# Gating of the normalised input moved from VectorE to GpSimd in a one-core attention kernel

## What is computed

```python
xn = jax.nn.silu(group_norm(x, gn_scale, gn_offset))
qkv = jnp.einsum('bxyc,cd->bxyd', xn, w_qkv)
q, k, v = jnp.split(qkv, 3, axis=-1)
...
q = q * HEAD_CH ** (-0.5)
sim = jnp.einsum('bhdi,bhdj->bhij', q, k)
attn = jax.nn.softmax(sim, axis=-1)
out = jnp.einsum('bhij,bhdj->bhid', attn, v)
...
out = jnp.einsum('bxyd,dc->bxyc', out, w_out) + b_out
return out + x
```

## Time and profile before

| | |
|---|---|
| device time, median of 3 runs | 3889.32 us (3886.81 to 3890.93) |
| the profiled execution, its device time | 3886.07 us |
| its span, first to last instruction | 3884.3 us |
| mean granted TensorE clock | 0.99 of full speed |
| busy: PE / PEld | 3643.0 us (94%) / 2099.6 us (54%) |
| busy: DVE | 3349.9 us (86%) |
| busy: ACT | 2811.0 us (72%) |
| busy: POOL | 1766.9 us (45%) |
| DMA, queue of the program's transfers | 21.2% of 16 engines' span |

### The profile page before, as it was taken

How to read it: one execution, slowest core, us unless ns; L and a number is a source line. 1 busy time by engine, 2 the same in 40 slices (tenths; PEclk the granted TensorE clock), 3 DMA queues, 4 the chain that set the end, 5 groups by cost and what they waited for, 6 DMA issues and landing times. The chain is left out here.

```text
span 3884.3 us, 92365 instructions
## 1 busy us (share of the span) xinstructions
PE 3643.0 (94%) x32844; PEld 2099.6 (54%) x32844; DVE 3349.9 (86%) x4378; ACT 2811.0 (72%) x3074; POOL 1766.9 (45%) x1739
## 2 busy tenths in 40 slices
PE   4889999999999999999999999999999999998997
PEld 2555555555555555555555555555555555555553
DVE  6888989889898898888888898888988989888885
ACT  3777777777777777777777777777777777777774
POOL 1353544445444444544535444344444444444444
PEclk7999999999999999999999999999999999999999
DMA  2212212132121222213122121221212222131220
GB/s 89 60 30 80 58 49 70 33 88 56 50 78 39 67 56 69 58 39 86 37 80 59 49 69 38 81 56 50 77 39 67 56 69 58 40 85 37 61 61 33
DMA packets 120769, 228.84 MB, mean 59 GB/s; under 512 B 12672, under 2 KB 29056, under 8 KB 120320
## 3 DMA queue, kind: packets, MB, share of 16 engines
q1 hardware_dynamic: 120320, 222.87, 21.2%
HBM read 71.57 MB, written 33.55 MB: 27 GB/s over the span
## 5 line engine op out<-in xcount | busy, mean ns | idle before, releaser
L509 POOL TENSOR_TENSOR Pl<-P,Ph 128x512 f16<-128x512 f32 x1024 | 1238.3, 1209 | 1703.9 <-ACT Ph L623 1691.0
L620 ACT ACTIVATE P<-ST,cns 128x1024 f32<-128x1024 f32 x1024 | 1141.0, 1114 | 899.3 <-PE ST L1108 883.4
L782 DVE TENSOR_REDUCE mx<-TP 128x1 f32<-128x1024 f32 x1024 | 1246.3, 1217 | 164.5 <-PE TP L1019 156.8
L623 ACT ACTIVATE Ph<-ST,cns 128x1024 f16<-128x1024 f32 x1024 | 1133.8, 1107 | 0.0
L835 DVE TENSOR_TENSOR Pl<-P,Ph 128x512 f16<-128x512 f32 x1024 | 978.8, 956 | 11.5 <-ACT Ph L623 7.3
L1137 PE MATMUL PV<-V,Ph 128*128 128x129 f16 (+2 forms) x10240 | 862.1, 210 | 3.9 <-DVE Pl L835 1.4
L1137 PEld LDWEIGHTS PV<-V,Ph 128*128 128x128 f16 x10240 | 772.0, 97 | 124.9 <-ACT pv_sum L631 8.8
L1137 PE MATMUL PV<-V,Pl 128*128 128x65 f16 x8192 | 834.8, 192 | 0.0
L1137 PEld LDWEIGHTS PV<-V,Pl 128*128 128x128 f16 x8192 | 723.0, 98 | 109.1 <-issue 0.6
L1108 PE MATMUL ST<-QK 128*128 128x512 f16 x2048 | 778.2, 380 | 2.6 <-issue 2.6
L1107 PE MATMUL ST<-QK 128*128 128x512 f16 x2048 | 778.6, 380 | 0.2 <-ACT Ph L623 0.2
(11 more groups left out here) (105 smaller groups left out, 2872.8 us busy)
## 6 DMA issues: line engine op xcount, KB each, us to landing
QK<-QK SPq DMA_DIRECT2D x384, 256.0 KB, 4.8
res<-in_x SPq DMA_DIRECT2D x128, 256.0 KB, 2.8
out<-res SPq DMA_DIRECT2D x128, 256.0 KB, 2.0
x_in<-in_x SPq DMA_DIRECT2D x61, 512.0 KB, 3.8
V<-V SPq DMA_DIRECT2D x16, 1040.0 KB, 6.3
V<-in_L_conv_w_qkv SPq DMA_DIRECT2D x4, 768.0 KB, 10.2
P<-in_L_conv_w_out SPq DMA_DIRECT2D x1, 1024.0 KB, 13.9
z<-in_x SPq DMA_DIRECT2D x1, 512.0 KB, 5.6
```

What stands on the lines that cost most here:

```text
L509: nc.gpsimd.tensor_tensor(Pl[:, v % 4, HALF:], P32[:, v % 2, HALF:], Ph[:, v % 4, HALF:], ALU.subtract).then_inc(lo_pool, 1)
L620: nc.scalar.activation(P32[:, v % 2, :], ST[:, slot, :], ACT.Exp, scale=cns[:, 0:1])
L623: nc.scalar.activation(Ph[:, v % 4, :], ST[:, slot, :], ACT.Exp, scale=cns[:, 0:1]).then_inc(exp_done, 1)
L782: nc.vector.reduce_max(mx[:, hh, qb:qb + 1], TP[:], AX.X).then_inc(top_drained, 1)
```

## The change

VectorE no longer takes part in the gating except in the prologue. GpSimd's new `silu` does four operations for each piece, with a semaphore `silu_step` between dependent ones: th = z th; high part of xn = z + th, written as float16; z = z + th, float32; low part = z - high part (this last is what `low_xn` did). `silu_ops(step, u)` deals them out from unit (1,10) on, alternately two and one in a unit: two in even units, one in odd ones, 32 operations in units (1,10) to (2,14). They stand behind `low_probs` and the division in GpSimd's queue. `Z_AT` and `TANH_AT` move to fit, and `silu_tanh` waits for the low part of the piece two before, because `th` is now read until then.

```diff
-Z_AT = [(1, 8), (1, 11), (1, 13), (2, 1), (2, 4), (2, 7), (2, 11), (2, 13)]
-TANH_AT = [(1, 9), (1, 12), (1, 15), (2, 3), (2, 5), (2, 9), (2, 12), (2, 15)]
-SILU_AT = [(1, 11), (1, 13), (2, 0), (2, 4), (2, 7), (2, 11), (2, 13), (3, 0)]
-LOW_XN_AT = [(1, 12), (1, 14), (2, 1), (2, 5), (2, 8), (2, 12), (2, 14), (3, 1)]
+Z_AT = [(1, 8), (1, 10), (1, 13), (1, 15), (2, 2), (2, 5), (2, 7), (2, 10)]
+TANH_AT = [(1, 9), (1, 11), (1, 14), (2, 0), (2, 3), (2, 6), (2, 8), (2, 11)]
+SILU_FROM = (1, 10)
...
+def silu_ops(step, u):
+
+    n = 16 * step + u - 16 * SILU_FROM[0] - SILU_FROM[1]
+    first = 3 * (n // 2) + 2 * (n % 2)
+    return [divmod(k, 4) for k in range(first, first + 2 - n % 2) if 0 <= k < 4 * PIECES]
...
+            def silu(image, par, i, op):
+
+                c, half = i % CC, i // CC
+                n = 3 * PIECES * (image - 1) + 3 * i
+                if op == 0:
+                    pool.wait_ge(silu_ready, PIECES * image + i + 1)
+                    nc.gpsimd.tensor_tensor(th[:, i % 2], z[:, i % 2], th[:, i % 2], ALU.mult).then_inc(silu_step, 1)
+                if op == 1:
+                    pool.wait_ge(silu_step, n + 1)
+                    nc.gpsimd.tensor_tensor(xn[:, par, c, half, 0], z[:, i % 2], th[:, i % 2], ALU.add
+                                            ).then_inc(silu_step, 1)
+                if op == 2:
+                    pool.wait_ge(silu_step, n + 2)
+                    nc.gpsimd.tensor_tensor(z[:, i % 2], z[:, i % 2], th[:, i % 2], ALU.add).then_inc(silu_step, 1)
+                if op == 3:
+                    pool.wait_ge(silu_step, n + 3)
+                    nc.gpsimd.tensor_tensor(xn[:, par, c, half, 1], z[:, i % 2], xn[:, par, c, half, 0],
+                                            ALU.subtract).then_inc(xn_lo, 1)
...
-                    if (s, u) in LOW_XN_AT and not last:
-                        low_xn(b + 1, 1 - par, LOW_XN_AT.index((s, u)))
+                    for i, op in [] if last else silu_ops(s, u):
+                        silu(b + 1, 1 - par, i, op)
...
-                wait(act, xn_f32, PIECES * image + i - 1)
+                wait(act, xn_lo, PIECES * image + i - 1)
...
-                        if (s, u) in SILU_AT:
-                            silu(b + 1, 1 - par, SILU_AT.index((s, u)))
```

More of the change, by code:

```diff
@@ L322, in conv_attention @@
         xn_f32 = sem("xn_f32")
+        silu_step = sem("silu_step")
         xn_hi = sem("xn_hi")
```

## The result

Before ran at 3888.07 us (median of 4), the changed kernel at 3820.22 us (3818.45 to 3822.49, 4 runs): ratio 0.9826, 95% interval 0.9809 to 0.9843. It is faster by 68 us, 1.7%; the forecast was 3833, 56 us less. The profiled execution took 3821.33 us around a span of 3819.6.

The account below looks back on a forecast made before the run. TensorE's work plus its waits, mainly for `ms` behind the port VectorE and GpSimd share, bounds the kernel. Release 6.3 us an image, less GpSimd's load, nets -3.7, times 15 = -56: 3886 - 56 = 3830, plus 3 gives 3833 us; range 3795 to 3905.

Parts of the forecast that it names:

- the gated stretch: Unit (1,10) to the end of (3,1), where the next image is gated; TensorE busy 84.25 of 91.00 us, losing 6.75.
- The rules of the port: Four rules on how VectorE and GpSimd operations delay each other at their shared port; a hand-over costs GpSimd about 0.38 us.
- the fourth: With both queues full, VectorE and GpSimd alternate at the shared port; shown for one tiny operation only.
- Rival 3: GpSimd keeps the port through back-to-back operations, delaying VectorE in even units: slower by 92 us, 3981; chance 0.15.
- The walk: Following VectorE's and GpSimd's queues through the stretch unit by unit with known durations: net -3.7 us an image.
- The price of the release: Taking the gating operations off VectorE shortens shift units and their neighbours by 6.3 us an image at most.
- rival 1: Port not crowded, VectorE's operations find gaps: the full 6.3 us x 15 = 94 us, 3795; chance 0.12.
- Unit (2,9) stays at 4.7: In (2,9), and (2,1) built like it, the transposed output delays VectorE, not gating, so the release gains nothing there.
- The average wait of `ms`: In shift units GpSimd is never idle, so `ms` waits for an operation's end: on average 0.6 us, at most 1.2.
- Rival 2: GpSimd becomes the bound, every operation colliding at 1.54 us: the stretch stays at 91 us, 3889; chance 0.13.
- GpSimd keeps up: A pair of units asks 7.1 us of GpSimd, which has 6.6 plus stalls; it holds, without much to spare.
- recovers at the long units: GpSimd falls behind by up to half a microsecond a pair and catches up at (2,1), (2,5) and (2,9).

## Why the prediction was right

*Where the time was lost, and by what.* Right: the gated stretch, and in it `ms` in the shift units. TensorE's wait for `ms` fell from 98.0 to 75.1 us over the whole run; the changed kernel's row:

```profile
PE TP L1050 <- DVE ms L778: 75.1, 98, 3.0
```

*The rules of the port.* Right, all four; the fourth rested on one four-element operation and now stands on full-size ones. VectorE's Pl never took more than one GpSimd operation (1.27 us) and 0.55, as its durations over the whole run of the changed kernel show (least, median, most, in ns):

```profile
L861 DVE TENSOR_TENSOR Pl<-P,Ph x1024: 670/855/1823, 104.9 to 3776.3; 128x512 f16<-128x512 f32 x171
```

Rival 3 (GpSimd keeps the port) did not occur. That the port is held for one instruction does not say who gets it next; these durations do. The gap between dependent operations of GpSimd, which the prediction set against this rival, is 0.07 us (from L512 to L515 in (2,5) of the experiment with the shift units spared), but VectorE was let in between independent ones too, which have none. One case in the changed kernel's 1024 shows the edge: a Pl issued 0.04 us before the end of one GpSimd operation found the next already in, and took 1.82 us.

*The walk.* It gave the sixth image 3.7 us, and the trace shows 3.8: (2,5) 4.55 against 4.6 measured, (2,9) 5.0 against 5.1, (2,12) to (2,14) 11.0 against 11.0, (3,1) 3.5 against 3.5. Two terms were off. (1,12) to (1,14) take 10.1 us, not 10.4, since `ms` of (1,13) met only the end of a GpSimd operation and took 0.42 us; and 0.2 us come back in (3,2), which the walk leaves out. These two nearly cancel. The sum also enters (2,9) with +0.2 where the walk has 4.7 to 5.0; this tenth is within its rounding. Times 15 it is 57 us, the forecast's 56.

*The price of the release, rival 1.* Wrong: 6.3 us an image and 94 in all, against 7.2 in the sixth image and 120 measured (some 7 of the 120 are the clock, below). The step that failed is "Unit (2,9) stays at 4.7, and (2,1), which is built like it, too: there the transposed output delays VectorE, and no gating does". In (2,9) the gating one unit earlier delayed `ms` by the 0.4 us that put it behind GpSimd's Pl; moving one table entry took a microsecond off. In (2,1) two gating operations stand at the head of the unit. It did not hurt the forecast, and that is partly luck: with the change `ms` meets a GpSimd operation in both units all the same (0.98 us long in each, the units 4.7 and 5.1), so that what the release gives there the load takes back. The prediction had both prices too small, the release by 0.9 us an image and the load by 0.8, and only their difference right.

*The average wait of `ms`*, "0.6 us and at most 1.2": right in size. In the sixth image `ms` takes 0.42, 0.98, 1.10, 0.98 and 0.91 us in (1,13) to (2,13), of which 0.23 are its own. But it is no matter of chance: nearly the same waits recur from image to image.

*The price of GpSimd's work.* Rival 2 sets "0.43 + 0.68 us on VectorE against four operations" of GpSimd. The low part among the four was GpSimd's before too; three were added.

*GpSimd keeps up*: right for TensorE's `times_v`, but the conclusion "recovers at the long units" hid that it is a unit late in between. That lateness is what made my own remedies fall short.

*The remaining 9 to 12 us* of the difference are not the walk's. The 2nd, 4th and so on to the 14th image save 3.8 us each, the 5th, 9th and 13th 4.4 to 4.5, the 3rd, 7th and 11th 6.0 to 6.2, the 15th 7.3, and the 1st only 1.4. In the 3rd, 7th, 11th and 15th the kernel before ran some of its matmuls at the lower clock. Two of these stretches, at the end of unit (1,8) of the 3rd and the 7th image, and then the whole steady run of the changed kernel (length, busy times, clock third from the end):

```profile
656.20:659.60 3.40, 3.40 (x10) 1.22 (x8) 1.45 (x3) 0.86 (x1) 0.00 (x0) 0.50 0.91 192
1598.30:1601.60 3.30, 3.30 (x10) 1.11 (x9) 2.13 (x3) 0.00 (x0) 0.00 (x0) 0.50 0.66 139
```

```profile
211.10:3747.20 3536.10, 3430.09 (x31386) 1993.19 (x31384) 3068.26 (x3875) 2684.66 (x2929) 2176.97 (x1994) 1.00 0.22 59
```

Before has four such stretches between 211 and 3747 us, each 3.3 to 3.4 us at 1.2 GHz (0.50) instead of 2.4, which costs some 1.7 us each: about 7 us. Ahead of the first three TensorE had stood idle 2.1 us in (1,8) for VectorE's drain of a projection (this wait: 29.0 us in all, 15 times, longest 2.1), ahead of the fourth 2.6 us in (2,0) of the 15th image. In the changed kernel the wait in (1,8) is 1.8 us in every image from the 2nd to the 15th and no drop follows. But the idle time alone does not decide: before idles the same 2.1 us in (1,8) of the 5th, 9th, 13th and 15th image and the changed kernel 2.6 us in (2,0) of the 15th, and the clock stays up. What decides stays open. The other 0.6 us of the odd images from the 3rd to the 13th stand in (1,8), where before is 0.3 us slower than in its even images, and in (2,1), where before is 0.2 slower and the changed kernel 0.15 faster; why stays open too. So these 7 us are a by-product and not a merit of the change.

## What to carry to other kernels

Count a shared port in the ends of operations, not in busy shares: a 0.23 us operation on the critical path costs 1.0 if the neighbour has just begun a 1.15 us one, and the fix is to let the neighbour wait for it, which here was worth 46 us before the change and 31 after it. Work moved to an idle engine lands where that engine's queue is at the time, not where the table says; check how late it is before choosing a place. Relief of an engine can be worth more than its time, where the time it gives back decides which side of another's start an operation falls on. And look at the clock when an experiment makes TensorE wait longer: about a quarter of what the added load cost here was matmuls at half clock, not the load.

## What the runs showed of the hardware

- VectorE operations with two inputs in SBUF, and a four-element one from SBUF to SBUF, wait for the running GpSimd operation: the first end 0.55 us after it, the last 0.02 to 0.03. GpSimd's wait for VectorE's and lose 0.38 to 0.46 us to each (1.54 instead of 1.16, 1.73 instead of 1.27). Row maxima from PSUM stay at 1.20 to 1.23 us throughout. Between two back-to-back operations of GpSimd, VectorE's Pl got its turn, unless it had been issued in the last hundredths of a microsecond of the first.
- GpSimd takes 1.26 to 1.27 us for a 128x512 operation of float32 inputs, whether the output is float32 or float16, and 1.15 to 1.16 with one float16 input.
- Moving work with nothing added or removed changed the time by 15 us, by one unit of one entry. The even images from the 2nd to the 14th repeat to within 0.05 us (before 234.83 to 234.87 us, changed 231.01 to 231.06).
- Every drop of TensorE's clock to 1.2 GHz between the 2nd and the 15th image, 4 in the kernel before and 18 with the load added, came after TensorE had stood idle for 2.0 to 2.6 us. Not every such idle time was followed by one; none of the 1.8 us ones was.
